# Both layers' local attention, gated products and the output in one run of slots

## The reference, cut to what matters

```python
def _layer(x, wqkv, qs, ksc, wo, lg, lb, w1, b1, w2, b2):
    h = shift_token(x)                       # upper half of the width from the token before
    q, k, v = jnp.split(h @ wqkv, 3, axis=-1)        # 8 heads of 64
    q, k = rotary_xpos(l2norm(q) * qs, l2norm(k) * ksc)
    o = local_attention(q, k, v)             # windows of 64, 128 keys each
    x = x + o @ wo
    h = shift_token(x)
    mu, var = h.mean(-1, keepdims=True), h.var(-1, keepdims=True)
    h = (h - mu) / jnp.sqrt(var + 1e-05) * lg + lb
    a, g = jnp.split(h @ w1 + b1, 2, axis=-1)        # 341 wide each
    return x + (a * jax.nn.gelu(g, approximate=False)) @ w2 + b2
for l in range(DEPTH):                       # DEPTH = 2
    x = _layer(x, ...)
return x_before + x                          # rows of the output
```

## Time and profile before

| What | us |
|---|---|
| median of 3 runs (1555.27 to 1565.25) | 1559.28 |
| the profiled execution's own time | 1561.78 |
| its span in the trace | 1559.7 |
| `clustered_attention` and `mlp_and_turn`, start to 703.2 | 703.2 |
| `local_attention`, layer 0 and layer 1 | 340.6 and 338.3 |
| `gated_ffn` with `clear` of layer 0; `gated_ffn` of layer 1 | 79.4; 79.5 |

### The profile page before, as it was taken

How to read it: one execution, slowest core, us unless ns; L and a number is a source line. 1 busy time by engine, 2 the same in 40 slices (tenths; PEclk the granted TensorE clock), 3 DMA queues, 4 the chain that set the end, 5 groups by cost and what they waited for, 6 DMA issues and landing times. The chain is left out here.

```text
span 1559.7 us, 27015 instructions
## 1 busy us (share of the span) xinstructions
PE 1302.9 (84%) x9156; PEld 604.5 (39%) x9156; DVE 1154.4 (74%) x1983; ACT 1032.9 (66%) x2355; POOL 787.6 (50%) x957
## 2 busy tenths in 40 slices
PE   3488989999899886786899999859778999998596
PEld 1122222222222221572555555533235555555243
DVE  5778878888888772234888888859458888887493
ACT  3246666666666665775889999852268899987422
POOL 4567666676675500225767777500077667774000
PEclk9569999999999999897999999979889999999698
DMA  3523333333433300101111111010011111110001
GB/s 97 108 55 62 62 68 62 72 61 58 75 62 63 67 2 1 54 1 38 25 25 27 30 25 25 19 44 0 14 32 25 25 25 25 32 25 12 1 1 55
DMA packets 161259, 60.87 MB, mean 39 GB/s; under 512 B 139706, under 2 KB 152932, under 8 KB 161124
## 3 DMA queue, kind: packets, MB, share of 16 engines
q1 hardware_dynamic: 161124, 59.15, 18.0%
HBM read 8.66 MB, written 2.10 MB: 7 GB/s over the span
## 5 line engine op out<-in xcount | busy, mean ns | idle before, releaser
L633 DVE TENSOR_REDUCE row_max<-max_ps 128x2 f32<-128x1024 f32 x256 | 312.9, 1222 | 71.0 <-PE max_ps L445 69.6
L685 ACT ACTIVATE prob<-scores_ps 128x1024 f32<-128x1024 f32 x256 | 262.0, 1023 | 148.4 <-PE scores_ps L425 144.9
L1668 POOL TENSOR_TENSOR la_turned<-la_raw,lw_rot 128x1024 f32<-128x1024 f32 x64 | 150.7, 2355 | 275.6 <-ACT la_raw L1560 146.0
L1549 ACT ACTIVATE la_s<-la_s,la_bias,la_inv 128x128 f32<-128x128 f32 x512 | 222.9, 442 | 8.2 <-DVE la_bias L1462 7.9
L1305 PE MATMUL la_ring<-lw_wqkv,la_hT 128*128 128x512 f32 x384 | 205.7, 647 | 24.8 <-ACT la_hT L1544 13.4
L425 PE MATMUL scores_ps<-stack 128*128 128x512 f16 x512 | 155.8, 386 | 41.5 <-ACT prob L685 40.8
L1674 POOL TENSOR_TENSOR la_turned<-la_turned,la_swapped 128x1024 f32<-128x1024 f32 x64 | 150.6, 2353 | 5.0
L459 PE MATMUL heads_ps<-prob,v_pad 128*32 128x512 f32 x1024 | 137.3, 608 | 1.1 <-ACT prob L685 1.1
L445 PE MATMUL max_ps<-stack 24*128 24x512 f16 x512 | 102.8, 398 | 31.8 <-DVE row_max L633 19.2
L1437 DVE TENSOR_TENSOR la_swapped<-la_ring,lw_rot 128x256 f32<-128x256 f32 x256 | 92.0, 416 | 32.6 <-ACT la_raw L1560 25.3
L425 PEld LDWEIGHTS scores_ps<-stack 128*128 128x128 f16 x512 | 34.2, 97 | 208.5 <-ACT prob L685 160.8
(11 more groups left out here) (170 smaller groups left out, 2727.3 us busy)
## 6 DMA issues: line engine op xcount, KB each, us to landing
la_v_back<-la_v_own SPq DMA_DIRECT2D x112, 128.0 KB, 2.3
X<-in_x SPq DMA_DIRECT2D x8, 256.0 KB, 5.0
stack<-stack_tok SPq DMA_TRANSPOSE x128, 3.2
out<-X SPq DMA_DIRECT2D x8, 256.0 KB, 2.4
lw_wqkv<-in_wqkv SPq DMA_DIRECT2D x2, 768.0 KB, 4.9
stack<-shift_row SPq DMA_DIRECT2D x64, 2.0 KB
lw_rot<-in_rot SPq DMA_DIRECT2D x2, 512.0 KB, 6.2
lw_w<-in_fw SPq DMA_DIRECT2D x2, 341.0 KB
```

The costliest lines, as they stand in the source:

```text
L633: nc.vector.tensor_reduce(row_max[:, grp % 2, w // 2, :, w % 2], max_ps[:], AX.X, ALU.max).then_inc(max_made, 1)
L685: nc.scalar.activation(prob[:, c % 4, 2 * pr:2 * pr + 2, :], scores_ps[:], ACT.Exp, scale=1.0 / LOGIT_SCALE).then_inc(exp_made, 1)
L1549: ins = nc.scalar.activation(s_ps[:, place(h), :], s_ps[:, place(h), :], ACT.Exp, bias=bias[:, T % 2, h:h + 1], scale=inv[:, T % 4, h:h + ...
L1668: nc.gpsimd.tensor_tensor(spun, raw[:, T % 2].rearrange("p s (h f) -> p s h f", f=LD), rot[:, T % TPB, :, 0, :].unsqueeze(2).to_broadcast( ...
```

## The change

`local_attention`, `gated_ffn`, `add_and_store` and `clear` become one function, `local_layers`, in one `Block` with one run of slots 0 to 86 for both layers. `slot_of(T)` puts tile T of layer 1 (T = 32 to 63) ten slots behind layer 0's; `ffn_slot(f)` puts batch f of the gated products four slots behind the last tile of its layer, so slots 35 to 42 and 77 to 84. The transposes back and the stores of the output run two slots behind, in slots 79 to 86, in place. Weights of layer 1 are loaded inside the run. The PSUM banks of the attention are used again (`chunk_banks`): two pairs for the products where three were.

The variance is now formed by tokens: four products with one column give 128x4, ACT adds epsilon, POOL raises it to the power -0.5 (`ALU.pow`, one 128x4 instruction for a batch), and in the batch's own time PE spreads it over the partitions (`spread_inverses`), DVE multiplies (`divide`) and ACT, no longer DVE, applies gain and bias (`take_hn`).

```diff
-        for layer in range(DEPTH):
...
-            local_attention(nc, a, layer, XT, Z[:].rearrange("p (b t) d -> p b (t d)", b=B), VAR, layer_w)
-            gated_ffn(nc, a, layer, XT, Z[:].rearrange("p (b t) d -> p b (t d)", b=B), VAR, layer_w)
-            clear(nc, taken)
...
-        add_and_store(nc, a, X, XT)
+        local_layers(nc, a, X, XT, Z[:].rearrange("p (b t) d -> p b (t d)", b=B), layer_w)
...
+        def slot_of(T):
+            return T + REST * (T // NT)
...
+        def ffn_slot(f):
+            return slot_of(f // B * NT + NT - 1) + 4 + f % B
...
+        def chunk_banks(j):
+            return ((ring_ps[:, 0, :], s_flat[:, 0:S]), (s_flat[:, S:2 * S], pT_flat[:, 0:S]))[j % 2]
...
+            def wait_for_products(layer):
+                if layer > 0:
+                    pe.wait_ge(gate_made, layer * B * NC)
+                    pe.wait_ge(prod_made, layer * B * NC)
+                    pe.wait_ge(divided, layer * B)
...
+            def spread_inverses(f):
+                pe.wait_ge(dev_inverted, f + 1)
...
+                for t in range(TPB):
+                    mm = nc.tensor.matmul(spread_ps[:, t * P:(t + 1) * P],
+                                          inv_dev[:, f % B, t:t + 1].to_broadcast([P, P]), ident[:],
+                                          start=True, stop=True)
+                mm.then_inc(spread, 1)
...
             def slot(n):
-                T, R, U, O = (tile_or_none(n - x) for x in (0, 2, 3, 4))
+                T, R, U, O = (tile_at(n - x) for x in (0, 2, 3, 4))
+                f, ahead, behind, end = (ffn_at(n - x) for x in (0, -1, 1, 2))
+                if f is not None:
+                    if O is not None:
+                        prob_turn(O, 0)
+                        prob_turn(O, 1)
+                    gated(f, 0)
+                    if O is not None:
+                        weigh(O, 0)
+                        weigh(O, 1)
+                        O = None
+                if ahead is not None and f is not None:
+                    spread_inverses(ahead)
+                if f is not None:
+                    gated(f, 1)
+                if end is not None and end >= BATCHES - B:
+                    turn_out(end)
+                if behind is not None:
+                    gated_out(behind)
+                if f is not None:
+                    gated(f, 2)
...
-                    nc.tensor.matmul(m_ps[:], mean_of[:], csq[:], start=True, stop=True
-                                     ).then_inc(m_filled, 1)
+                    for tile in range(TPB):
+                        mm = nc.tensor.matmul(m_ps[:, tile:tile + 1], csq[:, tile * P:(tile + 1) * P],
+                                              mean_of[:, 0:1], start=True, stop=True)
+                    mm.then_inc(m_filled, 1)
...
+            def divide(f):
+                c = batch_at(C, f)
+                dve.wait_ge(spread, f + 1)
+                nc.vector.tensor_tensor(c, spread_ps, c, ALU.mult).then_inc(divided, 1)
...
+            def take_hn(f):
+                act.wait_ge(divided, f + 1)
...
+                nc.scalar.activation(hn[:, f % 2, :], batch_at(C, f), ACT.Identity,
+                                     scale=ln[:, 0:1], bias=ln[:, 1:2]).then_inc(hn_made, 1)
...
-                    nc.scalar.activation(batch_at(VAR, b), m_ps[:], ACT.Copy).then_inc(var_made, 1)
+                    nc.scalar.activation(var[:, b % 2], m_ps[:, 0:TPB], ACT.Identity, bias=eps[:]
+                                         ).then_inc(var_made, 1)
...
+                b = ended(n - 8)
+                if b is not None:
+                    pool.wait_ge(var_made, b + 1)
+                    nc.gpsimd.tensor_tensor(inv_dev[:, b % B], var[:, b % 2], root[:], ALU.pow
+                                            ).then_inc(dev_inverted, 1)
```

More of the change, by code:

```diff
@@ L1125, with local_layers @@
 RING_TILES = 2 * TPB
-def local_attention(nc, a, layer, XT, C, VAR, weights):
-    tag = f"la{layer}_"
+HID = D * 4 * 2 // 3
+HC = [(c, min(P, HID - c)) for c in range(0, HID, P)]
+NC = len(HC)
+REST = 10
+def local_layers(nc, a, X, XT, C, weights):
+    tag = "la_"
     with ExitStack() as ctx:
@@ new lines, in gated_out @@
+            def gated_out(f):
+                pe.wait_ge(prod_made, NC * (f + 1))
+                if f % B == 0:
+                    pe.wait_ge(pT_high, (f // B + 1) * NT)
+                else:
+                    pe.wait_ge(f_added, f)
+                for i, (_, m) in enumerate(HC):
+                    mm = nc.tensor.matmul(f_ps, w2[0:m, i, :], prod[0:m, f % 2, i, :],
+                                          start=(i == 0), stop=(i == NC - 1))
+                mm.then_inc(f_filled, 1)
@@ L1405, in slot @@
                     weigh(O, 1)
+                if ahead is not None and f is None:
+                    spread_inverses(ahead)
             run(pe, slot)
@@ L1507, in slot @@
                     take_out(out)
+                if f is not None and O is not None:
+                    take_high(O)
+                if f is not None:
+                    multiply(f, 0)
+                if ahead is not None and f is not None:
+                    divide(ahead)
+                if f is not None:
+                    multiply(f, 1)
+                if end is not None and end >= BATCHES - B:
+                    add_out(end)
+                if behind is not None:
+                    add_products(behind)
+                if f is not None:
+                    multiply(f, 2)
                 if T is not None:
@@ L1512, in slot @@
                     maxima(U)
-                if O is not None:
+                if O is not None and f is None:
                     take_high(O)
@@ L1641, in slot @@
                     act.wait_ge(m_filled, m_count(b, SQUARE))
-                    nc.scalar.activation(batch_at(VAR, b), m_ps[:], ACT.Copy).then_inc(var_made, 1)
+                    if b - 1 > 0:
+                        act.wait_ge(dev_inverted, b - 1)
+                    nc.scalar.activation(var[:, b % 2], m_ps[:, 0:TPB], ACT.Identity, bias=eps[:]
+                                         ).then_inc(var_made, 1)
+                if ahead is not None and f is None:
+                    take_hn(ahead)
             run(act, slot)
```

379 lines of the change are left out of this document (165 added, 214 removed).

## The result

The changed kernel took 1510.03 us in the median of four runs (1507.15 to 1511.71), beside 1558.41 for the kernel before on the same chip: a ratio of 0.968, 95% interval 0.965 to 0.972. The forecast was 1514, range 1502 to 1529. Timed twice more beside the experiments it gave 1510.18 (ratio 0.966, 0.963 to 0.968) and 1508.47 (0.965, 0.963 to 0.967). The profiled execution took 1510.46, its span is 1508.7.

What follows compares the result with a forecast made beforehand. Bound: a ring through ACT, DVE and PE in steady attention, PE in gated batches, no full engine at the seams. -20.3 - 2.9 + 0.9 - 23.3 - 1.4 + 2.0 = -45.0, from 1559.28 to 1514.3 us; range 1502 to 1529.

Steps and rivals of the forecast that it cites:

- Steady attention, nothing: Steady attention slots: no change, as ACT's smaller copy only lengthens its wait and the one-column mean square takes about 0.9 us.
- The power: POOL's power in attention: costs nothing up to 3.1 us of cover, its time taken near the 128x16 row's 0.22.
- A: Attention: fourteen powers of 3.1 to 6.3 us each outlast their cover, costing up to 45 us, 1514 to 1559; chance 0.08.
- Rival B: Attention: powers hold up the slot's ring, slower than before, 1583 at 8 us each, over 1% from 7.5; chance 0.03.
- Seam of layer 0, -20.3: Layer 0's attention to gated stage: first gated product at about 1030.3 instead of 1050.59, saving 20.3 us.
- Gated stage of layer 0, -2.9: Layer 0's first gated product to layer 1's first projection: PE's queue takes 73.1 us instead of 76.0.
- Start of layer 1, +0.9: Layer 1's first projections: +1.9 for the last second product ahead, -1.0 for PE coming out of full work.
- seam of layer 1, -23.3: Layer 1's attention to gated stage: last tile's first turning to first gated product falls from 26.93 to 3.6 us.
- Gated stage of layer 1 and the end, -1.4: Layer 1's first gated product to the end of the span: 84.2 us instead of 85.6.
- The clock, +2.0: First gated products after each new seam: PE at 1.2 GHz takes some 1 us longer in each layer.
- C: Gated products: two pairs of banks instead of three bind, 3.1 us more a batch, 1564, or 1539 at half; chance 0.05.
- E: Seams: first gated product waits for the whole drain; only barriers, roots, inversions go, about 11 us each, 1537; chance 0.03.

Runs made afterwards that it cites:

- pow8: Changed kernel with eight powers a batch on POOL instead of one, seven into a spare buffer nobody reads: 1558.51 us, ratio 0.997.
- late8: Changed kernel with the gated stage eight slots later in both layers, behind the whole drain, so nothing overlaps: 1536.4 us, ratio 0.983.
- after_third: The changed kernel unaltered, timed a third time as the mark beside the repeat of the early projections: 1508.47 us, ratio 0.965.
- after_again: The changed kernel unaltered, timed once more as the common mark for three kernels beside it: 1510.18 us, ratio 0.966.
- pow4: Changed kernel with four powers a batch on POOL instead of one, three into a spare buffer nobody reads: 1507.47 us, ratio 0.966.
- out_last: Changed kernel with the eight output rows turned back and stored behind the last gated slot: 1520.29 us, ratio 0.972.
- early_proj: Changed kernel with layer 1's first Q and K projections ahead of turning back and second product, timed twice: 1506.8 and 1506.29 us.

## Why the prediction was right

It was right in the time and in most of what makes it, 4 us above the median. By the sum it is -45.0 against -48.4 between the medians and -51.0 between the profiled spans, of which the one before was 3.4 us over its median. The missing 6 lie in layer 1's attention (2.9), the clock (2.0), the end (0.8) and the stages ahead of the change (0.8, which it doesn't touch), less 0.4 of the first seam and stage.

*Steady attention, nothing:* right. Four slots take 37.5 us in both traces. The eight one-column passes of L1519 take 0.95 us, 0.12 each, as the weights' size had said. By the Trainium skill (TensorE: Matmul & The Clock Gate, Wait — 56ns, not 53.3ns?, the section ahead of the one that the prediction names) starts of small matmuls come down to some 25 ns; one column with weights of 128x128 doesn't come near it here.

*The power:* covered, as forecast, but at 1.02 us it is 4.6 times the 128x16 row and not near it, and the cover is 4.2 us, not 3.1. The count in rivals A and B was wrong too: of the sixteen powers ten, not fourteen, have a `spin` of attention behind them. Where the gain ends pow8 shows itself: eight powers, 7.8 us at the 0.98 each of its row, leave a ratio of 0.997. Rival B had a loss of over 1% from 7.5 us on; its formula makes 14 x 4.7 = 66 us of 7.8, and pow8 lost some 49, and even that only since PE's clock made up for part of the wider cover and the smaller count. By the Trainium skill (GPSIMD Engine Reference, Instruction dispatch) the first call to a freshly loaded kernel pays about 6 us. The first power here starts at 816.50, 1.00 behind the operation of 1.04 ahead of it, and has no such gap; whether its code was freshly loaded no run shows.

*Seam of layer 0, -20.3:* measured -20.0, link by link. `take_hn` took 0.81 for 0.65, the spreading 1.16 for 0.9, and from the start of the spreading to the first gated product it is 4.05 us (1025.75 to 1029.80) for the 4.3 forecast (1026.0 to 1030.3). One sign was worded wrong: the first gated product was to stand 3 to 5 us behind the last tile's first turning, and it stands 1.30 behind it (1028.50 to 1029.80). The 3.6 of the forecast were counted from where this turning stood before, while by its own links it moves back too, behind `divide`.

*Gated stage of layer 0, -2.9:* measured -2.8. The number is net: late8 shows -6.8 without overlap (no block ends, and the last second product moved behind, against the spreadings), and the overlap puts 4.1 back.

*Start of layer 1, +0.9, and seam of layer 1, -23.3:* together -22.4 forecast, -25.3 measured. The seam itself, from the last squares to the first gated product, gave 23.9 (53.34 to 29.47), and between first and last squares 0.6 were lost, in a slot that ran at the low clock. The start is the mis-sized term: -2.0 up to the first squares (11.38 to 9.38) instead of +0.9. The last second product is on the path as forecast, +1.7 for +1.9 (3.54 for 1.81 between the projection of the values and the next set). What was mis-sized is the clock: two sets of projections were at the low level before (3.75 and 3.68 us) and at the high one now (1.95 and 1.88), which gave 1.8 and 1.9, together 3.7, where I took 1.0 for one set. In after_third's layer 0, where no second product stands there and the second set runs high, the distance of the two rows is 1.81 again. Of the seam's 23.9 some are chance of the executions: before, layer 1's stretch was 3.8 longer than layer 0's (53.34 and 49.57), and in after_third the changed kernel's takes 27.09 at a granted clock of 1.00, 2.4 less than in the first profile.

*Gated stage of layer 1 and the end, -1.4:* measured -2.2. A gated slot takes 9.06 us for 9.1 (1473.58 to 1482.64), and the span ends 2.8 us behind DVE's last addition, where the forecast had 3.35 and the sign 3 to 4.

*The clock, +2.0:* measured 0 where it was put, at the first gated products, in the first profile, but after_again shows the same stretch at 0.66 and its gated stage 1.7 us longer (74.97). The low clock also falls where the forecast had none, in the drain ahead of the seam (0.90 and 0.89, above). The term exists in some executions and not in others; as a constant at one place it was the wrong form.

Of the rivals, C has no row (no pair waits for the bank; by its own terms a batch would be 3.0 longer, not 3.1), and E would be late8 or nearly so: put at 1537, measured 1536.4. That it came out so near is partly luck: I gave 11 us a seam to barriers, roots and inversion, while late8's trace has 2.7 and 4.3 in the seams and the rest at the blocks' ends and at layer 1's start. I had not seen that the token-wise variance costs 4 us in the old order. What it buys, I take it, is that a batch's normalisation is ready in its own time, so that a gated product can stand ahead of the drain; no kernel tried the new order without it.

What stays open is how the saving of 25 us without overlap splits between fewer blocks and the normalisation in a batch's own time; no kernel took one without the other in the new order.

## What to carry to other kernels

Look for time between stages before time inside them: laying two drains, in which no engine is full, over the stages behind them gave 28 us, and one block with each batch normalised in its own time nearly as much again. What goes into such a gap is free only until a wait further down runs out; the first wait that a profile shows is not yet a cost (pow4), and the real cover is found by adding work until the time moves. A step that costs more by itself (here 4 us) may pay if it frees the order, which no run here shows by itself.

## What the runs showed of the hardware that was not expected

A power of 128x4 on POOL takes 1.02 us, as long as a product of 128x512 there (1.04), while a 128x16 product takes 0.22. The cost of a chain in which PE mostly waits is paid twice: in pow8 and out_last two-pass or four-pass steps went from 1.02 to 1.91 and from 0.63 to 1.09 us. And the same program's start of attention ran once with three, once with one set of projections at the low clock (3.75, 3.68 and 3.52 us in the first profile; 3.75 and then 1.98 in after_third), and their stretches up to the first gated product differ by 3.2 us (323.96 and 320.77), more than early_proj brings.
